# Mixture of experts into attention on one core: layer two's first batch is mixed and normed inside the pass over the experts

## The chip, the cores and the metric

The kernel runs on one core of a Trainium2 chip, as one program. The metric is the device time in microseconds (us), the median over runs. The core's engines have a queue each: TensorE (PE, matrix products and turns, that is transposes through the identity), VectorE (DVE), ScalarE (ACT), GpSimd (POOL) and SyncE (SP, which here only issues DMAs). They meet through semaphores.

## The reference

Eight batches of 512 tokens, 256 wide, pass two layers, float32 throughout:

```python
x = x + attn0(layernorm(x))      # six heads, convolutions, a rotating state scanned over the tokens
x = x + ffn0(layernorm(x))       # sixteen experts, two for each token, and a shared one
x = x + attn1(layernorm(x))      # sixteen heads of 128, causal softmax
x = x + ffn1(layernorm(x))       # gated, 688 wide, weights looked up in a table of sixteen
```

What the change touches is the end of `ffn0` and the start of `attn1`. `ffn0` adds to each token the outputs of its two experts, each times the token's weight for it:

```python
for e in range(E):
    routed = routed + mask[..., e:e + 1] * _swiglu(x, wg[e], wu[e], wd[e])
```

## The kernel before

The first layer runs in four units of two batches. In it each token is given two slots, and GpSimd scatters the normed token to both of them in a DRAM tensor, `tokens_by_expert`, of 80 tiles of 128 slots (`NTILE`), sorted so that each tile belongs to one expert. Slots are given unit by unit, so those of unit 0, which holds batches 0 and 1, lie in the first tiles that were opened; the change reckons with 32.

**The pass over the experts** then takes the 80 tiles one by one. PE works in steps: turn of tile t (`tile_turn`), gate and up of tile t-1 (`tile_gate_up`), turn back of t-2 (`tile_turn_back`), down product of t-3 (`tile_down`). Every fourth step it also reads the numbers of the next four experts into registers. ACT copies each product out of the banks of PSUM and stores the results two tiles at a time (`store_tiles`) into `expert_results`; DVE multiplies gate by up (`tile_product`). Banks 0 and 1 are the turns', 2 and 3 gate and up, 4 and 5 the turn back, 6 and 7 the down product.

Beside its product DVE has a second job in each step: it unpacks the table weights of the second layer's feed-forward part (`unpack_to`). An entry is a comparison in bf16 (`unpack_equal`, equal<-fidx_bf) and a multiply-add (`unpack_add`, fws<-equal), both 128x544. There are 112 of them until the end of the pass, 30 before it starts; the last sixteen, of the late chunk, are left for the first heads of layer two.

**Behind the pass** stands the start of layer two for batch 0, in this order: all results stored (`stored`); eight gathers on GpSimd of the rows that batch 0 needs (`gather`, into `yg`); the mix and the statistics on DVE; the norm (`norm_chain_whole`, `norm_apply`); PE's eight turns of the normed `xn` into banks 6 and 7 (`turn`); ACT's and DVE's split of them into a high and a low part (`layer_norm_high`, `layer_norm_low`, h_high and h_low); and the products of q, k and v for head 0 (`make_qk`, `make_v`). PE fills its wait with turns of the identity (`clock_turns`), 200 and then 20, whose result is not read. Batches 1 to 7 have the same steps spread over the heads of the batch before, and are not touched.

GpSimd's part of the pass is the low half of five weight tiles (`low_qk_weights`, `low_v_weights`, `low_out_weights`), once ACT has copied their high halves in its turns 40 to 48. SP loads the tiles of tokens in pairs, index chunks, two sets of head weights, and x of batches 0 and 1 (`load_x`).

The order of the work on each engine is the order in which this code is written; no scheduler changes it.

## Time and profile before

| | us |
|---|---|
| median of 3 runs | 2196.58 |
| lowest, highest | 2193.62, 2198.37 |
| span of the profiled execution | 2190.4 |
| time of the profiled execution beside its span | not given by the page |
| PE busy | 2123.2 (97%) |
| DVE busy | 1694.3 (77%) |
| ACT busy | 1273.8 (58%) |
| GpSimd busy | 559.2 (26%) |

The span runs from the first to the last instruction of one profiled execution; the runs' times hold what lies around it as well. PE's share counts the fills as work. The shares are means over stages with different limits, so the change has to be read from its own stage, which is the pass (477 to 617 us of the span) and what stands behind it until about 642.

### The profile page before, as it was taken

The page shows a single profiled execution, that of the slowest core. Times are in us where ns is not written, and L with a number is a line of the kernel's source. Part 1 is how long each engine was busy: PE and PEld are TensorE (multiplying, and loading weights), DVE is VectorE, ACT ScalarE, POOL GpSimd, SP SyncE. Part 2 cuts the span into 40 slices and gives each one's busy share as a digit, 9 for nine tenths or more (in the row PEclk, how much of TensorE's full clock was granted, in tenths as well). Part 3 has the DMA queues.
Part 4 walks back from the last instruction along what each step waited for, and adds up shares of the span by engine and source line. Part 5 has one row for each costly group of instructions (what it writes and reads, how often), then busy time and mean ns, then how long its engine had stood idle before and what let it go on. Part 6 is the DMA issues. An engine that isn't in the chain of part 4 may idle for free. (4 is left out here: it accounts for less than half of the span.)

```text
span 2190.4 us, 37661 instructions
## 1 busy us (share of the span) xinstructions
PE 2123.2 (97%) x13038; PEld 1854.3 (85%) x13038; DVE 1694.3 (77%) x4387; ACT 1273.8 (58%) x3487; POOL 559.2 (26%) x604
## 2 busy tenths in 40 slices
PE   6899999979999999999999999999999999999997
PEld 5677777758788999899989989998998999899887
DVE  7998886887767887777876877787687778767775
ACT  5644443226637676666665666666566666656662
POOL 0214333430015323122222312222232222222220
PEclk9999999999999999999999999999999999999999
DMA  9001010436522112112111211211121121111100
GB/s 300 1 1 58 20 46 26 170 121 205 172 68 64 59 51 76 39 52 70 54 40 55 82 39 54 69 54 39 57 80 39 54 68 54 39 58 50 39 20 20
DMA packets 88556, 145.81 MB, mean 67 GB/s; under 512 B 8369, under 2 KB 55857, under 8 KB 88369
## 3 DMA queue, kind: packets, MB, share of 16 engines
q1 hardware_dynamic: 67904, 112.73, 16.1%
q0 software_dynamic: 6144, 16.79, 2.2%
q10 hardware_dynamic: 14320, 13.90, 1.9%
q8 instruction: 106, 1.74, 0.3%
q14 instruction: 82, 0.66, 0.1%
HBM read 105.63 MB, written 37.75 MB: 65 GB/s over the span
## 5 line engine op out<-in xcount | busy, mean ns | idle before, releaser
L1018 ACT ACTIVATE pr<-bank,negmax 128x128 f32<-128x128 f32 (+3 forms) x512 | 263.5, 527 | 196.6 <-DVE negmax L1599 196.6
L653 POOL TENSOR_TENSOR wo_low<-wraw_o,wo_high 128x256 fp32r<-128x256 f32 x128 | 94.5, 738 | 1105.0 <-ACT wo_high L705 1105.0
L1136 DVE TENSOR_TENSOR p_low<-bank,p_high 128x512 fp32r<-128x512 f32 (+2 forms) x384 | 190.2, 551 | 100.6 <-ACT p_high L705 100.0
L705 ACT ACTIVATE p_high<-bank 128x512 fp32r<-128x512 f32 (+2 forms) x384 | 177.4, 497 | 149.9 <-PE bank L2121 149.9
L1599 DVE CUSTOM_DVE_ANT_0 bank<-bank,causal 128x128 f32<-128x128 f32 (+3 forms) x512 | 234.7, 520 | 1.1 <-PE bank L1762 1.1
L1626 DVE SCALAR_TENSOR_TENSOR xs<-bank,rinv,xs 128x256 f32<-128x256 f32 x512 | 211.7, 474 | 1.2 <-PE bank L1762 1.2
L1760 PE MATMUL bank<-h_high,wqk_high 128*128 128x512 f32 x512 | 202.6, 396 | 0.0
L1761 PE MATMUL bank<-h_low,wqk_high 128*128 128x512 f32 x512 | 202.5, 396 | 0.0
L1762 PE MATMUL bank<-h_high,wqk_low 128*128 128x512 f32 x512 | 202.3, 395 | 0.0
L1136 DVE TENSOR_TENSOR z_low<-bank,z_high 128x512 fp32r<-128x512 f32 x128 | 88.4, 691 | 130.8 <-ACT z_high L705 130.3
L643 POOL TENSOR_TENSOR wqk_low<-wraw,wqk_high 128x512 fp32r<-128x512 f32 x128 | 165.6, 1294 | 77.3 <-ACT wqk_high L705 77.3
L2121 PEld LDWEIGHTS bank<-ident,pr 128*128 128x128 f32 x1280 | 147.6, 140 | 18.4 <-ACT pr L1018 1.3
L2121 PE MATMUL bank<-ident,pr 128*128 128x128 f32 x1280 | 160.4, 272 | 1.1 <-ACT pr L1018 1.1
L705 ACT ACTIVATE z_high<-bank 128x512 fp32r<-128x512 f32 x128 | 76.6, 599 | 138.1 <-PE bank L2132 138.1
L1760 PE MATMUL bank<-wv_high,h_high 128*128 128x256 f32 x512 | 154.8, 302 | 0.0
L1760 PE MATMUL bank<-wo_high,z_high 128*128 128x256 f32 x512 | 148.0, 289 | 2.4 <-issue 2.3
L1762 PE MATMUL bank<-wv_high,h_low 128*128 128x256 f32 x512 | 144.5, 282 | 0.0
L1762 PE MATMUL bank<-wo_high,z_low 128*128 128x256 f32 x512 | 144.1, 282 | 0.0
L1761 PE MATMUL bank<-wv_low,h_high 128*128 128x256 f32 x512 | 144.0, 281 | 0.0
L1761 PE MATMUL bank<-wo_low,z_high 128*128 128x256 f32 x512 | 143.8, 281 | 0.0
L1760 PE MATMUL bank<-k_high,q_high 128*128 128x384 f32 (+2 forms) x384 | 140.8, 367 | 0.0
L1760 PE MATMUL bank<-p_high,v_high 128*128 128x512 f32 (+2 forms) x384 | 131.2, 342 | 2.4 <-DVE p_low L1136 2.3
(338 smaller groups left out, 6327.3 us busy)
## 6 DMA issues: line engine op xcount, KB each, us to landing
wraw<-in_wpair SPq DMA_DIRECT2D x64, 512.0 KB, 4.0
wraw<-in_wpair SPq DMA_DIRECT2D x64, 256.0 KB, 4.4
wraw_o<-in_wpair SPq DMA_DIRECT2D x64, 256.0 KB, 2.5
tokens_by_expert<-zero SPq DMA_DIRECT2D x10, 1024.0 KB, 11.2
xt<-tokens_by_expert SPq DMA_DIRECT2D x40, 256.0 KB, 3.3
expert_results<-ey ACTq DMA_DIRECT2D x40, 256.0 KB, 3.7
wres<-in_wexp SPq DMA_DIRECT2D x1, 6144.0 KB, 20.7
xs<-x_between_stages SPq DMA_DIRECT2D x8, 512.0 KB, 4.5
```

The costliest lines, as they stand in the source:

```text
L643: pool.tensor_tensor(low, wraw[r][:, 2 * e * D:2 * (e + 1) * D], high.bitcast(F32), ALU.subtract).then_inc(s_wq, 1)
L653: pool.tensor_tensor(wo2[e][1][:], wraw_o[r][:, e, :], wo2[e][0][:].bitcast(F32), ALU.subtract).then_inc(s_wo, 1)
L705: sc.activation(dst, src, ACT.Copy, scale=scale).then_inc(done, 1)
L1018: ins = sc.activation(pr[:, i, 0:(i + 1) * P], score(i), ACT.Exp, scale=-1.0, bias=negmax[:, i:i + 1], accum_out=rsum[:, i:i + 1])
L1136: v.tensor_tensor(at(parts[1]), src, high_, ALU.subtract).then_inc(done, 1)
L1599: ins = v.tensor_tensor_reduce(score(i), score(i), causal[:, (NT - 1 - i) * P:NT * P], -1.0, -NEG, ALU.add, ALU.min, negmax[:, i:i + 1])
L1626: ins = v.scalar_tensor_tensor(xb[:, i, :], bank[6 + n][:, (i % 2) * D:(i % 2 + 1) * D], rinv[:, i:i + 1], xb[:, i, :], ALU.mult, ALU.add)
L1760: mm(dst, w[0], x[0], start=start, stop=False)
L1761: mm(dst, w[0], x[1], start=False, stop=False)
L1762: return mm(dst, w[1], x[0], start=False, stop=stop)
L2121: ins = pe.transpose(bank[2 + n][:, at:at + P], pr[:, i, j * P:(j + 1) * P], ident[:])
```

## The change

- The gathers of batch 0 wait for 32 stored tiles instead of all, and stand on GpSimd ahead of its five low weights. They read from the first 32 tiles of `expert_results` only.
- The mix of batch 0 goes from DVE to GpSimd: a multiplication of the gathered rows in place and an addition to x, four of each for each of the two experts, each waiting for the one before.
- DVE takes the statistics, the links of the norm and its application in pieces, one behind each tile from tile 56 on (`first_batch`).
- PE turns the normed batch behind the gate and up of the last tile, into banks 0 and 1; ACT and DVE split it in their turn there.
- All fills behind the pass are gone, the 200 and the 20.
- DVE's entries are spread anew over the pass (`entries_until`): 82 instead of 77 fall into it, and in the twelve tiles with a piece of the norm they come half as often. The five late entries behind the pass are gone.
- x of batch 0 is loaded at pair 12 instead of 24. The places of `yg` and of h2 for the even batches in SBUF are exchanged with others, so that they lie outside of what the pass uses. ACT's wait for all stores moves behind its copies of q, k and v.

```diff
-LATE_ENTRIES = 5
+LATE_ENTRIES = 0
+FIRST_TILES = 32
+FIRST_STATS = 56
+FIRST_CHAIN = FIRST_STATS + 4
+FIRST_APPLY = FIRST_CHAIN + 4
...
+            first_tiles_stored(pool)
+            for n in range(2 * NT):
+                gather(0, n)
+            pool.wait_ge(s_x1[0], 16)
+            for c in range(2):
+                for i in range(NT):
+                    if c == 0:
+                        pool.wait_ge(s_yg[i], 32)
+                    linked(pool.tensor_scalar(yg[:, i, c, :], yg[:, i, c, :], wts[:, i, c:c + 1], None, ALU.mult))
+                for i in range(NT - 1):
+                    linked(pool.tensor_tensor(xs[0][:, i, :], xs[0][:, i, :], yg[:, i, c, :], ALU.add))
+                pool.tensor_tensor(xs[0][:, NT - 1, :], xs[0][:, NT - 1, :], yg[:, NT - 1, c, :], ALU.add
+                                   ).then_inc(s_mix, 1)
+                pool.wait_ge(s_mix, c + 1)
             low_qk_weights(0, 0, 0)
...
             stored(pool)
-            for n in range(2 * NT):
-                gather(0, n)
...
+            def first_batch(t):
+                n = t - FIRST_STATS
+                if 0 <= n < NT:
+                    if n == 0:
+                        v.wait_ge(s_mix, 2)
+                    ins = v.bn_stats(stats[:, n, :], xs[0][:, n, :])
...
+                n = t - FIRST_CHAIN
+                if 0 <= n < 4:
+                    norm_chain(2, 0, n)
+                n = t - FIRST_APPLY
+                if 0 <= n < NT:
+                    ins = v.tensor_scalar(xn[:, n, :], xs[0][:, n, :], mv[:, n, 0:1], ry[:, n:n + 1],
+                                          ALU.subtract, ALU.mult)
...
+            def entries_until(t):
+                busy = min(max(t + 1 - FIRST_STATS, 0), FIRST_APPLY + NT - FIRST_STATS)
+                weight = 2 * (t + 1) - busy
+                return (LATE_CHUNK * LUTN - early) * weight // (2 * NTILE - FIRST_APPLY - NT + FIRST_STATS)
...
+            for t in range(NTILE):
+                tile_product(t)
+                unpack_to(early + entries_until(t))
+                first_batch(t)
+            layer_norm_low(2, 0, h2[0], 0)
...
+                if t == NTILE:
+                    turn(2, 0, 0)
```

The first place is PE at the end of the pass. L2040 is gate and up, L2047 the turn back, L2053 the down product, ISA an instruction that reads the expert's number from a register. Before:

```order
L2040 MATMUL bank<-wres,xT 128x256
L2047 MATMUL bank<-ident,eh 128x128
L2053 ISA
L2053 MATMUL bank<-wres,ehT 128x256
L2047 MATMUL bank<-ident,eh 128x128
L2053 ISA
L2053 MATMUL bank<-wres,ehT 128x256
L2053 ISA
L2053 MATMUL bank<-wres,ehT 128x256
L1931 MATMUL bank<-ident 128x128 x200
L2099 MATMUL bank<-ident,xn 128x128 x8
L1931 MATMUL bank<-ident 128x128 x20
```

Now, with the lines of the changed kernel (L2072 is gate and up, L2079 the turn back, L2085 the down product, L2114 the turns of xn):

```order
L2072 MATMUL bank<-wres,xT 128x256
L2114 MATMUL bank<-ident,xn 128x128 x8
L2079 MATMUL bank<-ident,eh 128x128
L2085 ISA
L2085 MATMUL bank<-wres,ehT 128x256
L2079 MATMUL bank<-ident,eh 128x128
L2085 ISA
L2085 MATMUL bank<-wres,ehT 128x256
L2085 ISA
L2085 MATMUL bank<-wres,ehT 128x256
L1792 MATMUL bank<-h_high,wqk_high 128x512
```

The eight turns stand in front of two turns back and three down products, and the first product of layer two directly behind the last of these.

The second place is ACT at the same point: ey is the result of a tile, h_high the high part of the normed batch. Before:

```order
L927 ACTIVATE esg<-bank 128x128
L933 ACTIVATE ehT<-bank 128x128
L940 ACTIVATE ey<-bank 128x256
L944 DMA expert_results<-ey 128x2x256
L933 ACTIVATE ehT<-bank 128x128
L940 ACTIVATE ey<-bank 128x256 x2
L944 DMA expert_results<-ey 128x2x256
L705 ACTIVATE h_high<-bank 128x512 x2
```

Now:

```order
L947 ACTIVATE esg<-bank 128x128
L953 ACTIVATE ehT<-bank 128x128
L960 ACTIVATE ey<-bank 128x256
L725 ACTIVATE h_high<-bank 128x512 x2
L964 DMA expert_results<-ey 128x2x256
L953 ACTIVATE ehT<-bank 128x128
L960 ACTIVATE ey<-bank 128x256 x2
L964 DMA expert_results<-ey 128x2x256
```

The two high copies now stand in front of the last tile's turned copy (ehT), on which PE's last down product waits.

The third place is GpSimd, from the last scatters of the first layer on. Before:

```order
L583 DMA tokens_by_expert<-xm,slots 10240x256 x21
L643 TENSOR_TENSOR wqk_low<-wraw,wqk_high 128x512 x2
L649 TENSOR_TENSOR wv_low<-wraw,wv_high 128x512 x2
L653 TENSOR_TENSOR wo_low<-wraw_o,wo_high 128x256
L669 DMA yg<-expert_results,slots 128x256 x8
```

Now:

```order
L591 DMA tokens_by_expert<-xm,slots 10240x256 x21
L677 DMA yg<-expert_results,slots 128x256 x8
L689 TENSOR_SCALAR yg<-yg,wts 128x256 x4
L691 TENSOR_TENSOR xs<-xs,yg 128x256 x3
L692 TENSOR_TENSOR xs<-xs,yg 128x256
L689 TENSOR_SCALAR yg<-yg,wts 128x256 x4
L691 TENSOR_TENSOR xs<-xs,yg 128x256 x3
L692 TENSOR_TENSOR xs<-xs,yg 128x256
L651 TENSOR_TENSOR wqk_low<-wraw,wqk_high 128x512 x2
```

The gathers and sixteen operations of the mix now stand ahead of the low weights.

## Rows read from the trace of the kernel before

**Rows 1.** The page: its first line, and a row of DMA issues.
```profile
span 2190.4 us, 37661 instructions
...
wraw<-in_wpair SPq DMA_DIRECT2D x64, 512.0 KB, 4.0
```

**Rows 2.** Stretches: us, then busy us (instructions) by engine, granted clock, DMA.
```profile
580.00:600.00 20.00, 20.00 (x109) 16.38 (x108) 15.46 (x38) 13.21 (x49) 0.00 (x0) 1.00 0.56 159
...
621.00:642.00 21.00, 21.00 (x190) 20.66 (x189) 10.73 (x35) 1.09 (x2) 7.49 (x8) 1.00 0.32 102
...
440.00:445.00 5.00, 2.90 (x22) 1.30 (x20) 4.55 (x15) 1.34 (x3) 0.00 (x0) 1.00 0.00 0
```

**Rows 3.** Timeline, 613 to 642: start, us, engine, line, operation [idle before, releaser].
```profile
613.13 1.03 PE L2040 MATMUL bank<-wres,xT 128*128 x4
...
614.50 0.29 DVE L1524 TENSOR_TENSOR eh<-esg,bank 128x128 f32<-128x128 f32 x1
...
616.77 0.39 ACT L940 ACTIVATE ey<-bank 128x256 f32<-128x256 f32 x1 [0.59 <-PE bank L2053]
...
617.18 0.37 ACTq L944 DMA_DIRECT2D expert_results<-ey  x1
...
620.84 1.02 POOL L669 DMA_INDIRECT yg<-expert_results,slots  x1 [57.91 <-DMA expert_results<-ey]
...
636.94 1.38 DVE L1591 TENSOR_SCALAR xn<-xs,mv,ry 128x256 f32<-128x256 f32 x4
...
638.46 1.06 PE L2099 MATMUL bank<-ident,xn 128*128 128x128 f32 x8
...
639.65 1.09 ACT L705 ACTIVATE h_high<-bank 128x512 fp32r<-128x512 f32 x2 [22.49 <-PE bank L2099]
640.27 1.29 DVE L1136 TENSOR_TENSOR h_low<-bank,h_high 128x512 fp32r<-128x512 f32 x2 [1.96 <-ACT h_high L705]
...
641.71 0.47 PE L1760 MATMUL bank<-h_high,wqk_high 128*128 128x512 f32 x1
```

**Rows 4.** Tile xt, whole run: ns min/median/max, first and last start; landing.
```profile
L2034 PE MATMUL bank<-ident,xt x160: 272/273/323, 477.1 to 611.6; 128*128 128x128 f32 x160
...
DMA to landing us min/median/max: 2.7/3.3/5.7
```

**Rows 5.** Timeline, the product and entries on DVE, and the turn back.
```profile
604.78 0.29 DVE L1524 TENSOR_TENSOR eh<-esg,bank 128x128 f32<-128x128 f32 x1 [0.31 <-ACT esg L927]
...
605.90 0.27 PE L2047 MATMUL bank<-ident,eh 128*128 128x128 f32 x1
...
617.81 0.30 DVE L1398 TENSOR_SCALAR equal<-fidx_bf 128x544 bf16<-128x544 bf16 x1
...
618.84 0.29 DVE L1398 TENSOR_SCALAR equal<-fidx_bf 128x544 bf16<-128x544 bf16 x1
```

**Rows 6.** Timeline, 549 to 553, around GpSimd's second weight difference.
```profile
549.11 0.62 ACT L705 ACTIVATE wqk_high<-wraw 128x512 fp32r<-128x512 f32 x1
...
549.81 1.36 POOL L643 TENSOR_TENSOR wqk_low<-wraw,wqk_high 128x512 fp32r<-128x512 f32 x1 [1.98 <-ACT wqk_high L705]
...
550.43 0.90 DVE L1398 TENSOR_SCALAR equal<-fidx_bf 128x544 bf16<-128x544 bf16 x1
...
552.57 0.32 PE L2047 MATMUL bank<-ident,eh 128*128 128x128 f32 x1 [1.06 <-DVE eh L1524]
```

**Rows 7.** Groups on GpSimd: busy us, mean ns, idle before.
```profile
L653 POOL TENSOR_TENSOR wo_low<-wraw_o,wo_high 128x256 fp32r<-128x256 f32 x128 | 94.5, 738 | 1105.0 <-ACT wo_high L705 1105.0
...
L583 POOL DMA_INDIRECT tokens_by_expert<-xm,slots x64 | 65.1, 1017 | 50.4 <-DVE slots L1349 32.4 <-issue 17.8
L669 POOL DMA_INDIRECT yg<-expert_results,slots x64 | 61.2, 957 | 72.7 <-DMA expert_results<-ey 57.9 <-issue 11.4
...
L615 POOL TENSOR_SCALAR shift<-upto,tilenos 128x16 f32<-128x16 f32 x3 | 1.0, 322 | 0.3
```

**Rows 8.** Timeline, the first head: ACT's weight copy.
```profile
657.05 0.62 ACT L705 ACTIVATE wqk_high<-wraw 128x512 fp32r<-128x512 f32 x1
```

More of the change, by code:

```diff
@@ L215, in two_layer_program @@
         fw2 = split("fw2", [P, FW])
-        h2 = [split(f"h2{i}", [P, KD, T]) for i in range(2)]
+        h2_odd = split("h21", [P, KD, T])
         f2 = split("f2", [P, KD, T])
-        yg = sb("yg", [P, NT, 2, D])
         q2 = split("q2", [P, T])
@@ L222, in two_layer_program @@
         v2 = [split(f"v2{i}", [P, NT, 2, DH]) for i in range(2)]
+        yg = sb("yg", [P, NT, 2, D])
+        h2 = [split("h20", [P, KD, T]), h2_odd]
         pr = sb("pr", [P, NT, T])
@@ L384, in stored, with first_tiles_stored @@
                 engine.wait_ge(s_yst[i], 16 * NTILE // 8)
+        def first_tiles_stored(engine):
+            for i in range(4):
+                engine.wait_ge(s_yst[i], 16 * FIRST_TILES // 8)
         def first_layer_over(engine):
@@ L669, in gather @@
                 pool.indirect_dma_start(
-                    yg[:, i, c, :], None, ysort,
+                    yg[:, i, c, :], None, ysort[0:FIRST_TILES * P, :] if b == 0 else ysort,
                     bass.IndirectOffsetOnAxis(ap=slots[:, b * NT + i, c:c + 1], axis=0)).then_inc(s_yg[i], 16)
+            first_tiles_stored(pool)
[12 more added lines that the diff above has]
+                pool.wait_ge(s_mix, c + 1)
             low_qk_weights(0, 0, 0)
@@ L1081, in head @@
                     store_out(b - 1)
-            stored(sc)
-            layer_norm_high(2, 0, h2[0], 6)
             high_q(0)
@@ L1088, in _ @@
             high_v(1, bank[2][:])
+            stored(sc)
             for g in range(NG):
@@ L1518, in _ @@
             v.tensor_copy(expert_row[:], bank[7][0:1, 0:NTILE]).then_inc(s_row, 1)
-            def tile_product(t):
-                v.wait_ge(s_es, t + 1)
-                if t >= 2:
-                    v.wait_ge(s_eu, t - 1)
-                v.tensor_tensor(eh[t % 2][:], esg[t % 2][:], bank[2 + t % 2][:, P:2 * P], ALU.mult).then_inc(s_ea, 1)
-            early = sum(EARLY_ENTRIES)
-            unpack_to(early)
-            for t in range(NTILE):
-                tile_product(t)
-                unpack_to(early + (t + 1) * (LATE_CHUNK * LUTN - LATE_ENTRIES - early) // NTILE)
-            unpack_to(LATE_CHUNK * LUTN)
             def low_q(g):
@@ L2055, in tile_down @@
                    ).then_inc(s_ed, 1)
-            experts = []
-            for t in range(NTILE + 3):
-                if t < NTILE:
-                    tile_turn(t)
-                if 0 <= t - 1 < NTILE:
-                    tile_gate_up(t - 1, experts[t - 1])
-                if t < NTILE and t % NVALUES == 0:
-                    experts += nc.values_load_multi_w_load_instructions(
-                        expert_row[0:1, t:t + NVALUES], engines=(mybir.EngineType.PE,), min_val=0, max_val=NEXP - 1,
-                        bass_reorder=False)[1]
-                if 0 <= t - 2 < NTILE:
-                    tile_turn_back(t - 2)
-                if 0 <= t - 3 < NTILE:
-                    tile_down(t - 3, experts[t - 3])
-            clock_turns(CLOCK_TURNS[5])
-            stored(pe)
             def make_qk(g):
@@ L2093, in make_v, with turn @@
                 ins.then_inc(s_v, 1)
-            def turn(n, b):
+            def turn(n, b, bank0=6):
                 pe.wait_ge(s_xn[n], b + 1)
@@ L2231, in head @@
                     scores(g + 1)
-            turn(2, 0)
-            clock_turns(NORM_TURNS)
+            experts = []
+            for t in range(NTILE + 3):
+                if t < NTILE:
+                    tile_turn(t)
+                if 0 <= t - 1 < NTILE:
+                    tile_gate_up(t - 1, experts[t - 1])
+                if t == NTILE:
+                    turn(2, 0, 0)
+                if t < NTILE and t % NVALUES == 0:
+                    experts += nc.values_load_multi_w_load_instructions(
+                        expert_row[0:1, t:t + NVALUES], engines=(mybir.EngineType.PE,), min_val=0, max_val=NEXP - 1,
+                        bass_reorder=False)[1]
+                if 0 <= t - 2 < NTILE:
+                    tile_turn_back(t - 2)
+                if 0 <= t - 3 < NTILE:
+                    tile_down(t - 3, experts[t - 3])
             make_qk(0)
```

34 lines of the change are left out of this document (16 added, 18 removed).

## The prediction

> **What bounds the kernel now.** I read the page first, for the span, 2190.4 us [rows 1]. The list of the last chain is of no use here, since it names no stretch, so I went to the stretches by time. In the pass over the experts TensorE (PE) is busy for all 20 us of 580 to 600, DVE for 15.5 and GpSimd for none [rows 2]. So PE sets the pace there, and DVE has about a quarter of its time free. Between 621 and 642 us PE is again busy for all 21 us, but with 190 instructions that are the fills (turns of the identity whose result nobody reads): this is a wait painted as work [rows 2]. The timeline says what the wait is for. The last expert product of gate and up starts at 613.13; the last results are stored from 617.18 and have landed by 620.84, when GpSimd's first gather starts; the mix and the norm on DVE go on to the four applications at 636.94; PE turns them at 638.46, ACT and DVE split them, and the first product of layer two starts at 641.71 [rows 3]. The reader is to see one serial chain of 28.6 us from 613.13 to 641.71, in which PE does nothing useful after about 616.7.
>
> **The change, part by part.** *The chain in front of the mix.* It now starts when 32 tiles are stored. PE's turns of the tiles go from 477.1 to 611.6 for 80 tiles, so 1.70 us a tile [rows 4]; tile 35, in whose ACT turn the sixteenth pair's store stands, is at 536.6, the store a little behind it at 537.5. With the 3.7 us from the last store to the gather, 617.18 to 620.84 [rows 3] the gathers start at 541.2. Eight of them at 0.957 and about 0.3 between them [rows 7] are 10.0 us: 551.2.
>
> *The mix on GpSimd.* Eight multiplications and eight additions of 128x256, each waiting for the one before. An addition has its row in the weight difference of that shape, 0.738. The multiplication by a column has none of this width. From below it is 0.32, the row of 16 columns; from above 1.06, that row and the two-input row of 256 columns added. I take 0.84, nearer to the row of the same width. With 0.1 idle behind each (0.3 over three in the row of 16 columns) [rows 7] the mix is 8 x 0.84 + 8 x 0.94 = 14.2 us, to 565.4; the ends are 10.1 and 16.0 us.
>
> *The low weights,* now behind it on GpSimd: four of 1.36 at most [rows 6] and one of 0.74 are 6.2 us, to 571.6. They are wanted at the first product of layer two, 47 us later: no cost.
>
> *The norm in DVE's turns 56 to 67.* PE turns tile 56 at 572.3 and DVE comes to its product two tile steps later, near 575.6. The mix is done 10 us before. Four statistics, sixteen small links and four applications (1.38 together [rows 3]) are about 7 us, spread over twelve tiles in which the new rule gives up half of the unpacking. Of this nothing reaches PE.
>
> *Unpacking.* DVE ends all 112 entries within the pass, five more than before, and eight tiles now have two entries. An entry takes 1.03, a product 0.29 [rows 5]. A double tile is thus 0.2 + 2.06 + 0.1 = 2.4 against the 1.70 of the step: the next product is 0.7 late. A product that starts at 604.78 is read at 605.90 in this rhythm, so about 0.8 is free, and 0.4 a tile is regained. Seven double tiles cost nothing or 0.2 each; that at tile 46 also has the cast of a new chunk and stands within the mix. I put down 0.5 us.
>
> *Contention.* While GpSimd works on a tensor, DVE's comparison in bf16 is held: GpSimd's difference runs from 549.81 for 1.36 us, the comparison that started at 550.43 took 0.90 in place of 0.30, and ended 0.15 behind it [rows 5, 6]. The multiply-add behind it is not held. From 551 to 571 GpSimd is at tensors nearly all the time, so each of some 13 comparisons loses on average a quarter of a microsecond with 0.8 us operations, and 0.5 with the longer ones at the end. A tile then takes 1.34 + 0.3, still below 1.70. I put down 0.5 us for what is left, above all at tile 46.
>
> The Trainium skill ("SBUF — State Buffer", section "SBUF: two separate sides") says the same of the cause: one port pair is shared by DVE and GpSimd, as a lock for a whole instruction, and not as a share of bandwidth. By this rule the held comparisons would wait and the others not, and the trace agrees. The section adds what speaks against this change: a DMA that GpSimd itself issues cannot write its descriptors while DVE holds the pair, 620 ns alone and about 3100 ns beside a DVE copy. With 3.1 us for each gather the mix would end at 580, and the sum would be 18 instead of 22. The row that bears on it, GpSimd's scatters, with DVE's comparisons beside part of them, has a mean of 1.017 against 0.957 of the gathers [rows 7], which shows little of it; I keep the rows' price.
>
> *The tail.* PE's last gate and up end at 614.16. Eight turns behind them (1.06 [rows 3]) end at 615.1, the turn back and down product of older tiles at 615.7. ACT's queue then has a result of 0.39, ending at 616.1, the two high halves (1.09, to 617.2), and one more short copy, 617.5; only then can PE do the last down product, which ends near 618.4. DVE's product of the last tile is at 614.50, its two entries end at 616.8, and the two low halves (1.29) behind the high ones end at 618.2 [rows 3]. Both paths meet at 618.4, where before there stood 641.71: **23.3 us**. The fills are gone, and PE stands idle for about 2 us at 616 to 618. Between 440 and 445 PE is busy for 2.90 of 5.00 us and the granted clock stays at 1.00, its upper level, 2.4 GHz [rows 2], so I put nothing on it.
>
> *What is late next.* The last result now leaves ACT near 618.8, the stores have landed by 622.5, and the next weight load, which waits for them as the first gather did at 620.84, is issued at 622.9. It feeds ACT's copy that stood at 657.05 and will stand at 633.8: 10.9 us for a load of 512 KB, which takes 4.0 by the page's row for these loads [rows 1, 8]. ACT's own wait for the stores now stands behind its copies of q, k and v, which need two rounds of products after 618.4 first; 622.5 is close to that, and I put nothing on it. *The earlier load of x* at the pair 12: the tile loads have landed in 5.7 us at worst [rows 4], and the next tile pair is asked for six tiles, 10 us, ahead. Its half megabyte and the megabyte of gathers are hidden by that.
>
> **Sum.** 23.3 saved in the tail, 1.0 given back in the pass: 22.3 us. The span would be 2168.1. The page gives no time for the profiled execution beside its span; the span is 6.2 us under the median of the runs, 2196.58, and I carry this over: 2174.3 us.
>
> **Rivals.**
> *Contention eats the pass.* If each of 13 comparisons lost the full 0.6 seen, that is 7.8 us; about 0.35 a tile is free, 4.2 over twelve tiles, and 0.8 once: 2.8 us. There are two PE idles of 1.0 already now near GpSimd's work, one at 552.57 in front of a turn back; I read them as ACT's, whose weight copy at 549.11 pushes the tile's own copy back just before PE reads its expert numbers [rows 6]. If they are GpSimd's, one or two more come: up to 4.8 in all. The price over the 1.0 already counted is 1.8 to 3.8, and the time 2176 to 2178. For it speaks the held row; against it that most of a tile's DVE work isn't held.
>
> *The mix is late.* DVE would stand at tile 56 with the last products behind it, and the PE loop with it. From 575.6 on each microsecond costs one. With 3.1 us a gather it is 4.4: 2178.7. By the rows it ends 10 us earlier.
>
> *Slower than before.* The same wait at tile 56, if GpSimd's operations got through only once in a DVE hold each. It decides from a mix that ends at 575.6 + 22.3 = 598, or 2.9 us for each of sixteen operations instead of 0.89; with 3.5 it is 10 us more, 2206. The weight difference of 512 columns, beside DVE's work, took 1.36 [rows 6], less than twice the 0.738 mean of 256 columns over the whole program, so GpSimd is hardly held.
>
> *The change doesn't do what it says:* the first product waits for something else that the fills hid, the weights or the stores, and stays near 641: 2197. I find nothing that is not ready by 623.
>
> **How the numbers follow.** The forecast has 0.73, contention 0.14, the late mix 0.06, no effect 0.02, slower 0.03, and 0.02 is a gain above 24.5 us. The forecast's own range is 2171.5 to 2176, with 1.5 us for the spread of the runs (2193.62 to 2198.37). To hold 8 in 10 I take in contention and most of the late mix, and the run spread below: 2171 to 2179.5. A measurement tells about 0.2%, 4.4 us, from no change: faster 0.95, same 0.02, slower 0.03.
>
> **What would show it.** In the changed kernel's profile: eight gathers near 541; sixteen GpSimd operations of 0.5 to 0.9 ending by 567; comparisons of up to 0.9 among them; no DVE wait for xs at its first statistics near 576; the eight turns of xn directly behind the last gate and up, near 614 to 616; the first product of layer two near 619, and the later stages shifted by the same amount. The two 1.0 idles of PE near 552 and 560 stay if they are ACT's. Wrong would be: a DVE wait for GpSimd at tile 56, several new PE idles between 550 and 572, the clock below 1.00 behind 616, or a wait for a weight load in the first head.

## The result and the profile after

| | before | changed |
|---|---|---|
| median, us | 2197.47 (4 runs, 2193.62 to 2199.59) | 2177.61 (4 runs, 2175.25 to 2182.67) |
| span of the profiled execution | 2190.4 | 2173.5 |

The ratio is 0.9916, with a 95% interval of 0.9904 to 0.9928: the change makes the kernel faster by 0.84%. The forecast was 2174.3, with a range of 2171 to 2179.5. The span of the profiled execution fell by 16.9 us where 22.3 were forecast, so a quarter of the gain is missing, and the study is about that quarter. The median came nearer to its forecast than the span did; how that came about stands under the sum at the end.

The page of the changed kernel, its first line and the busy times of the engines:

```profile
span 2173.5 us, 37227 instructions
PE 2102.6 (97%) x12818; PEld 1830.9 (84%) x12818; DVE 1694.2 (78%) x4379; ACT 1274.5 (59%) x3487; POOL 575.1 (26%) x620
```

PE's busy time is 20.6 us less, in the main the fills; GpSimd's is 15.9 more, the mix. DVE's sum is the same within 0.1 though the mix has left it: a DVE instruction that GpSimd's work holds up ("held" below) shows a longer time and counts as busy for all of it. A better first question than the totals is in which stage the time went. I cut the span at four starts: PE's first turn of a tile, the last gate and up, the first product of layer two, and ACT's first z_high (the high half of the first attention output).

| stage | before | changed | difference | forecast |
|---|---|---|---|---|
| up to the first turn | 477.1 | 477.4 | +0.3 | 0 |
| the pass, to the last gate and up | 136.03 | 141.23 | +5.2 | +1.0 |
| from there to layer two's first product | 28.58 | 5.08 | -23.5 | -23.3 |
| from there to z_high | 16.41 | 17.44 | +1.0 | 0 |
| the rest | 1532.28 | 1532.35 | +0.1 | 0 |

Up to the first turn both kernels do the same work there, but that stretch takes from 477 to 486 us in the executions below. The last stage, the rest, takes from 1532.1 to 1533.9 us in them. So single spans can't be compared to a microsecond; the three stages between can. The pass of the changed kernel took 141.23, and 141.07 and 141.15 in two other executions with the same pass.

**The tail.** The timeline of the changed kernel around the last gate and up: start, us, engine, line, operation, and in brackets the idle time before it with its releaser, as in [rows 3].

```profile
618.63 1.03 PE L2072 MATMUL bank<-wres,xT 128*128 x4
...
619.50 1.04 PE L2114 MATMUL bank<-ident,xn 128*128 128x128 f32 x8
...
621.87 0.60 ACT L725 ACTIVATE h_high<-bank 128x512 fp32r<-128x512 f32 x1
622.28 1.28 DVE L1157 TENSOR_TENSOR h_low<-bank,h_high 128x512 fp32r<-128x512 f32 x2
...
622.78 0.69 PE L2085 MATMUL bank<-wres,ehT 128*128 x2 [0.99 <-ACT ehT L953]
...
623.71 0.47 PE L1792 MATMUL bank<-h_high,wqk_high 128*128 128x512 f32 x1 [0.23 <-DVE h_low L1157]
```

The reader is to see that both paths of the forecast are there. PE waits 0.99 us for ACT's late ehT, and then 0.23 for DVE's low halves. Put on the forecast's clock (gate and up at 613.13), the first product stands at 618.21; 618.4 was forecast.

**Behind the tail.** ACT's rows of the changed kernel, and then of the one before, around its first exponentials of layer two:

```profile
632.86 1.28 ACT L1040 ACT_TABLE_LOAD   x1 [2.54 <-DVE negmax L1607]
634.15 0.37 ACT L1040 ACTIVATE pr<-bank,negmax 128x128 f32<-128x128 f32 x1
```

```profile
648.33 1.28 ACT L1018 ACT_TABLE_LOAD   x1
650.78 0.37 ACT L1018 ACTIVATE pr<-bank,negmax 128x128 f32<-128x128 f32 x1 [1.17 <-DVE negmax L1599]
```

Before, ACT loaded the table of the exponential while it would have waited for the maxima anyway, and still waited 1.17 us behind the load. Now the load begins only when the maxima are there, and its 1.28 us are all on the path.

**GpSimd in the pass.** Its timeline in the changed kernel, from the first gather on:

```profile
540.90 0.98 POOL L677 DMA_INDIRECT yg<-expert_results,slots  x1 [69.27 <-DMA expert_results<-ey]
...
550.69 4.80 POOL L689 TENSOR_SCALAR yg<-yg,wts 128x256 f32<-128x256 f32 x4
555.57 2.35 POOL L691 TENSOR_TENSOR xs<-xs,yg 128x256 f32<-128x256 f32 x3
...
559.18 4.16 POOL L689 TENSOR_SCALAR yg<-yg,wts 128x256 f32<-128x256 f32 x4
563.43 2.70 POOL L691 TENSOR_TENSOR xs<-xs,yg 128x256 f32<-128x256 f32 x3
566.20 0.73 POOL L692 TENSOR_TENSOR xs<-xs,yg 128x256 f32<-128x256 f32 x1
567.01 2.92 POOL L651 TENSOR_TENSOR wqk_low<-wraw,wqk_high 128x512 fp32r<-128x512 f32 x2
569.89 3.03 POOL L657 TENSOR_TENSOR wv_low<-wraw,wv_high 128x512 fp32r<-128x512 f32 x2
572.88 1.21 POOL L661 TENSOR_TENSOR wo_low<-wraw_o,wo_high 128x256 fp32r<-128x256 f32 x1
```

The gathers start within 0.3 us of the forecast. The mix runs from 550.69 to 566.9 (forecast 551.2 to 565.4). A row of four multiplications takes 4.80 and 4.16 us with the gaps between them; one alone takes 0.92 to 1.38, 1.05 on the mean. GpSimd is at tensors without a gap from 550.69 to 574.1.

**What DVE and PE do meanwhile.** The timeline of the changed kernel beside the low weights:

```profile
568.83 1.67 DVE L1429 SCALAR_TENSOR_TENSOR fws<-equal,luts,fws 128x544 f32<-128x544 bf16 x1
...
570.43 0.28 DVE L1751 TENSOR_TENSOR eh<-esg,bank 128x128 f32<-128x128 f32 x1
570.63 1.17 DVE L1419 TENSOR_SCALAR equal<-fidx_bf 128x544 bf16<-128x544 bf16 x1
570.76 0.33 PE L2079 MATMUL bank<-ident,eh 128*128 128x128 f32 x1 [1.02 <-DVE eh L1751]
...
571.83 1.67 DVE L1429 SCALAR_TENSOR_TENSOR fws<-equal,luts,fws 128x544 f32<-128x544 bf16 x1
...
573.75 0.33 PE L2079 MATMUL bank<-ident,eh 128*128 128x128 f32 x1 [1.01 <-DVE eh L1751]
```

An entry is an unheld comparison of 0.30 and a multiply-add of 0.79 elsewhere (the comparison in [rows 5]). Here both are held, 1.17 and 1.67, and with the product a tile takes DVE 3.0 us. PE's turns back stand 2.99 us apart, at 570.76 and 573.75. The product itself, which reads one input out of PSUM, takes its 0.28.

**PE's other idles in the pass.** The turns back of the changed kernel that had over 0.4 us in front of them, the two above left out:

```profile
546.13 0.32 PE L2079 MATMUL bank<-ident,eh 128*128 128x128 f32 x1 [0.56 <-issue]
...
554.11 0.33 PE L2079 MATMUL bank<-ident,eh 128*128 128x128 f32 x1 [1.08 <-DVE eh L1751]
...
562.00 0.32 PE L2079 MATMUL bank<-ident,eh 128*128 128x128 f32 x1 [0.99 <-issue]
...
599.54 0.33 PE L2079 MATMUL bank<-ident,eh 128*128 128x128 f32 x1 [0.44 <-issue]
```

The idles at 554 and 562 are the two of before ([rows 6] has the first). Those at 546 and 599 are new, and no GpSimd instruction on a tensor runs at either. I laid the turns back of both kernels beside each other and took the difference of their times tile by tile. Beyond the later start of the pass it grows by 0.4 in the first turns, where an entry now stands in turn 0; by 0.8 at 546; by 0.7 over 565.8 and 567.8, beside the mix's additions; by 2.7 from 570.8 to 575.6, beside and just behind the low weights; and by 0.6 at 599. These are 5.2 us, the difference of the stages.

### The profile page after: what moved, and what is told of

It is laid out like the page before. It is cut to its first block and busy times, and to the rows that moved or that the text cites. A ratio compares the mean times of both kernels' runs of the same rounds, so it can differ in the third digit from the quotient of the medians.

```text
span 2173.5 us, 37227 instructions
## 1 busy us (share of the span) xinstructions
PE 2102.6 (97%) x12818; PEld 1830.9 (84%) x12818; DVE 1694.2 (78%) x4379; ACT 1274.5 (59%) x3487; POOL 575.1 (26%) x620
## 3 DMA queue, kind: packets, MB, share of 16 engines
q1 hardware_dynamic: 67904, 112.73, 16.2%
```

## The experiments

The theory: the missing time is (a) entries held beside the low weights and the mix, 3 to 3.5 us; (b) entries that make a product late just before a turn in which PE reads expert numbers into registers, about 1.5 to 2 with the entry in turn 0; (c) the table load behind the stores' wait, 1.0. The rival for (a) is that the gathers' DMA or the placement of the entries slows the pass, and GpSimd's tensor work only stands beside it.

**1. The wait for the stores one step earlier.** The forecast put ACT's wait at nothing. The order of instructions shows what it became: the table load is made directly in front of the first exponential, and waits that stand between the last copy and the exponential come ahead of the load. ACT's row in the order, changed kernel, then kernel before:

```
L1040 ACT_TABLE_LOAD [waits tiles_stored3,tiles_stored2,score_max_bank,tiles_stored1]
L1018 ACT_TABLE_LOAD
```

The exponential now needs five waits, four for the stores and one for the maxima. It keeps one of the stores'; the other four, the one for the maxima among them, have gone ahead of the load. The edit:

```diff
             high_v(0, bank[5][:])
-            high_v(1, bank[2][:])
             stored(sc)
+            high_v(1, bank[2][:])
```

> The changed kernel with one edit: ACT's wait for all stores stands in front of the second copy of v instead of behind it. In the changed kernel the table load of the exponentials starts at 632.86, behind the first row maxima, and the first exponential at 634.15; the lead at the first product of layer two is 18.0 us against the kernel before, and 17.0 from the first head's z on. Theory: the wait for the stores, put directly ahead of the exponentials, drags the wait for the row maxima in front of the table load, so 1.28 us of loading are no longer hidden. Then here the load stands before 631.7, the first exponential 1.1 us behind the first row maximum, and the span is 1.0 us shorter, 2172.5. Rival: the load is late because ACT itself is late there (stores landing at 626); then the span stays at 2173.5 and the load stays behind the maxima.

The load then stands in the order with no wait at all, and ACT's timeline reads:

```profile
634.35 1.28 ACT L1040 ACT_TABLE_LOAD   x1
...
636.80 0.37 ACT L1040 ACTIVATE pr<-bank,negmax 128x128 f32<-128x128 f32 x1 [1.17 <-DVE negmax L1607]
```

From layer two's first product to z_high it took 16.52 us instead of 17.44, and the 1.17 of before is back. The span, 2178.0, isn't the 2172.5 expected: its pass began at 481.4 instead of 477.4, and its last stage took 1533.85 instead of 1532.35, a length that kernels without this edit reach too (1533.74 in experiment 5). (c) holds by its stage: 0.9 us.

**2. Low weights ahead of the gathers.** ACT's five copies go to turns 20 to 30, and GpSimd's five differences stand in front of the gathers:

```diff
+            low_qk_weights(0, 0, 0)
...
+            low_out_weights(0, 0, 0)
             first_tiles_stored(pool)
...
-                if t in (40, 42):
-                    high_qk_weights((t - 40) // 2)
+                if t in (20, 22):
+                    high_qk_weights((20, 22).index(t))
```

> The changed kernel with the five weight copies on ACT in turns 20, 22, 24, 28, 30 instead of 40 to 48, and GpSimd's five low weights ahead of the gathers, so that they run one at a time and not back to back behind the mix. The count of copies just before a register read is the same. Theory: GpSimd's operations of 1.3 to 1.5 us back to back hold both the comparison (1.17 instead of 0.30) and the multiply-add (1.67 instead of 0.79) of an entry, so two steps of 2.99 us stood in the pass between 567.8 and 573.8; here these two steps are 1.63 to 1.85 long and the first product of layer two is 2.3 to 2.6 us earlier (span 2170.9 to 2171.2); the two idles of 1.0 move to about 518 to 532. Rival: the two long steps come from DVE's own load, double entries and the cast; then they stay, and the span is within 0.5 us of 2173.5.

The pass took 138.64, 2.6 less, and both steps of 3 us are gone. The two idles of 1.0 have moved with ACT's copies, to 524.08 and 538.83. The differences now come singly, and DVE's and GpSimd's timeline shows what one alone does:

```profile
518.11 1.69 POOL L651 TENSOR_TENSOR wqk_low<-wraw,wqk_high 128x512 fp32r<-128x512 f32 x1 [41.67 <-ACT wqk_high L725]
...
518.79 1.17 DVE L1419 TENSOR_SCALAR equal<-fidx_bf 128x544 bf16<-128x544 bf16 x1
...
520.00 0.79 DVE L1429 SCALAR_TENSOR_TENSOR fws<-equal,luts,fws 128x544 f32<-128x544 bf16 x1
```

The comparison is held and the multiply-add isn't, since GpSimd is done by then. That is what stood in [rows 6] too, and it is why the forecast took the multiply-add for one that can't be held.

**3. ACT's weight copies off the register reads.** The copies of turns 42 and 46 go to 41 and 45:

```diff
-                if t in (40, 42):
-                    high_qk_weights((t - 40) // 2)
-                if t in (44, 46):
-                    high_v_weights((t - 44) // 2)
+                if t in (40, 41):
+                    high_qk_weights((40, 41).index(t))
+                if t in (44, 45):
+                    high_v_weights((44, 45).index(t))
```

> The changed kernel with ACT's weight copies in turns 40, 41, 44, 45, 48 instead of 40, 42, 44, 46, 48: none of them now stands two turns behind a register read's turn. Theory: the two PE idles of 1.0 us at 554.1 and 562.0 (552.57 and 560.47 before the change) come from a copy that delays the tile's own copy just ahead of the four expert numbers being read; both vanish and the span is 2.0 to 2.3 us shorter, near 2171.3. Rival: they are GpSimd's, through DVE's held entries; then both stay and the span does not move by more than 0.4.

The pass took 139.28, 1.95 less, just under the 2.0 to 2.3 expected. The first idle is gone: PE's turns back pass its place in steps of 1.6 to 1.8 (the row of 553.97 and the one behind it are a turn with a register read):

```profile
552.34 0.27 PE L2079 MATMUL bank<-ident,eh 128*128 128x128 f32 x1
...
553.97 0.31 PE L2079 MATMUL bank<-ident,eh 128*128 128x128 f32 x1
...
555.80 0.27 PE L2079 MATMUL bank<-ident,eh 128*128 128x128 f32 x1
```

At the second place an idle of 0.42 stays, one turn later, at 563.23, behind the turn that has two entries and the cast of a new chunk beside the mix. So the two idles were ACT's and not GpSimd's, though the profile names DVE as releaser of one of them, and 0.4 at the second place is DVE's. DVE's product is only the next in the row: it waits for the copies behind ACT's late one.

**4. No mix.** The gathers stay; the sixteen operations of the mix are left out, so that batch 0 goes on without its experts' outputs:

```diff
-            for c in range(2):
...
+            for i in range(NT):
+                pool.wait_ge(s_yg[i], 32)
+            pool.sem_inc(s_mix, 2)
```

> The changed kernel without the mix of batch 0: the gathers stay, GpSimd's eight multiplications and eight additions are left out (so batch 0 goes on without its experts' outputs), the low weights follow at once. Theory: the mix costs the pass the slow steps at 565.8 and 567.8 (0.7 us) and pushes the low weights into one block (2.5 us); without it these come one by one as before the change, and the first product of layer two is 3.0 to 3.4 us earlier (span 2170.1 to 2170.5); what stays against the pass before is 0.7 at its start, 0.8 at 546.1 and 0.6 at 599.5. Rival: the loss in the pass is DVE's own, entries and norm pieces; then the span moves by less than 1 us.

The pass took 137.97, 3.3 less. Without the mix the low weights are differences with gaps, as ACT delivers them. The gathers and the entries are still there, so neither the gathers' transfers nor the place of the entries alone costs these 3.3; (a) holds against its rival.

**5. Entries off the register reads.** No entry in turn 0; two entries only in turns of the form 4k+1 (9, 13, 17, 25, 37, 45, 53, 69, 77), and in the twelve turns of the norm one in six of them:

```diff
+            doubles = (9, 13, 17, 25, 37, 45, 53, 69, 77)
+            ones = (57, 58, 59, 61, 65, 66)
...
             def entries_until(t):
...
+                return sum(entries_of(n) for n in range(t + 1))
```

> The changed kernel with only DVE's entries spread otherwise: none in turn 0 as before the change, and the two-entry turns at 9, 13, 17, 25, 37, 45, 53, 69, 77, that is always just after a turn of number 4k, and the entries beside the norm pieces in turns 57, 58, 59, 61, 65, 66; 82 in all as before. Theory: every fourth turn PE's queue reads four expert numbers into registers and has no time to spare there, so a late product only costs when it is the one of turn 4k+1; this explains 0.8 us at 546.1 (behind the double turn 36) and 0.6 at 599.5 (behind turn 64 with cast and application); both idles vanish and the pass from first turn to last gate and up is 139.0 to 139.8 us long against 141.2. Rival: any late product costs, wherever the double turns stand; then the idles only move and the pass is 140.8 us or longer.

The pass took 139.59, 1.5 less than the 141.07 of the changed kernel on the same chip, and the idles at 546 and 599 are gone. A new one came: the double turn 45 falls into the mix's additions with the cast of a new chunk, and PE waits 1.46 us for its product at 568.19. Behind the low weights stands another of 0.61, at 584.67.

**6 and 7. All four together, with the mix on GpSimd and on DVE.** Both have the edits of 1, 2, 3 (weight copies in turns 20, 21, 24, 29, 28) and 5. The second takes the mix off GpSimd; DVE does it as one instruction for each gathered block, in eight turns that read no registers and hold no norm:

```diff
+            MIXES = (45, 46, 48, 49, 50, 52, 53, 54)
...
+                    ins = v.scalar_tensor_tensor(xs[0][:, i, :], yg[:, i, c, :], wts[:, i, c:c + 1], xs[0][:, i, :],
+                                                 ALU.mult, ALU.add)
```

> All four edits together: stores' wait in front of the second copy of v, weight copies on ACT in turns 20, 21, 24, 28, 29 (none two turns before a register read's turn end), low weights ahead of the gathers, entries as in the run of the entries alone. If the four causes are separate, their gains add: pass 134.3 to 135.2 us (141.2 less 2.6, 2.0 and 1.5 to 2.2), first product to first z 16.5 instead of 17.4, so 7.0 to 7.8 us below the changed kernel on the same chip, and 0.9880 to 0.9890 of the kernel before. If they overlap (the same slack counted more than once) the gain is under 6 us.

> As the run with all four edits, but the mix of batch 0 done by DVE as before the change, one of its eight operations (0.48 us) in each of the turns 45, 46, 48, 49, 50, 52, 53, 54, and GpSimd left with the gathers. Theory: GpSimd's operations hold the entries beside them, which costs the pass about what DVE's own eight would (4 us of DVE work, most of it in free time), so the pass is within 0.7 us of that with the mix on GpSimd. Rival: DVE is the bound in these turns, and each operation adds its 0.48 less 0.3 of free time to the pass: 1.5 us longer or more. Other rival: GpSimd's hold is what still costs, and without it the pass is 0.8 us shorter or more.

> The changed kernel itself once more, beside the others on one chip: pass 141.2 us, first product to first z 17.4, ratio to the kernel before 0.9916 within its interval. It gives the spread of the stage lengths between executions, expected at 0.1 us in the pass and up to 5 us in where the pass starts.

All three ran on one chip, with the kernel before at 2196.39 (9 runs):

| | median (lowest, highest), us | ratio to before, 95% | pass | to z_high |
|---|---|---|---|---|
| changed | 2180.77 (2179.97, 2181.12) | 0.9927 (0.9914 to 0.9941) | 141.07 | 17.42 |
| all four, mix on GpSimd | 2174.67 (2169.53, 2175.96) | 0.9894 (0.9875 to 0.9913) | 136.88 | 16.50 |
| all four, mix on DVE | 2172.67 (2172.38, 2175.32) | 0.9890 (0.9875 to 0.9906) | 135.56 | 16.49 |

By their medians the mended kernels are 6.1 and 8.1 us faster than the changed one. Of that the pass and the stage behind the tail carry 5.1 and 6.4, and another 0.3 is in the tail, 4.82 us in both; the rest lies in the spread of the stages that no edit touches. The sum of the four gains, 7.0 to 7.8, was missed. With the mix on DVE the pass is 0.5 shorter than in the kernel before, though it holds more entries and the whole mix; but that kernel still had its two idles of 1.0. It is 1.3 shorter than with the mix on GpSimd, where within 0.7 was expected: the second rival held, by which GpSimd's hold is what still costs.

With the mix on GpSimd the pass missed its expected 134.3 to 135.2 by 1.7 at least. That lies in two places. The first is new in both mended kernels: the copies of turns 20 and 21 come so close that GpSimd's first two differences, from 516.90 to 518.30 and from 518.52 on, follow each other, and a tile's two instructions are held again, 0.94 and 1.88. Two steps of PE take 2.20 and 2.22 instead of 1.63, 1.2 us in all:

```profile
518.49 1.88 DVE L1429 SCALAR_TENSOR_TENSOR fws<-equal,luts,fws 128x544 f32<-128x544 bf16 x1
518.52 1.27 POOL L651 TENSOR_TENSOR wqk_low<-wraw,wqk_high 128x512 fp32r<-128x512 f32 x1 [0.22 <-ACT wqk_high L725]
...
520.62 0.33 PE L2087 MATMUL bank<-ident,eh 128*128 128x128 f32 x1 [0.41 <-DVE eh L1759]
```

The second is the turn of experiment 5's new idle. DVE, GpSimd and PE there in the kernel with all four edits:

```profile
560.61 2.70 POOL L696 TENSOR_TENSOR xs<-xs,yg 128x256 f32<-128x256 f32 x3
...
561.53 1.19 DVE L1429 SCALAR_TENSOR_TENSOR fws<-equal,luts,fws 128x544 f32<-128x544 bf16 x1
...
562.64 0.96 DVE L1401 CAST fidx_bf<-fidxs 128x544 bf16<-128x544 int32 x1
563.38 0.80 POOL L697 TENSOR_TENSOR xs<-xs,yg 128x256 f32<-128x256 f32 x1
563.64 0.70 DVE L1419 TENSOR_SCALAR equal<-fidx_bf 128x544 bf16<-128x544 bf16 x1
564.28 4.37 POOL L694 TENSOR_SCALAR yg<-yg,wts 128x256 f32<-128x256 f32 x4
564.38 0.67 DVE L1426 TENSOR_SCALAR fws<-equal,luts 128x544 f32<-128x544 bf16 x1
564.97 0.27 DVE L1759 TENSOR_TENSOR eh<-esg,bank 128x128 f32<-128x128 f32 x1
...
565.30 0.33 PE L2087 MATMUL bank<-ident,eh 128*128 128x128 f32 x1 [1.83 <-DVE eh L1759]
```

Four held instructions in a row, 3.5 us, and PE waits 1.83. With the mix on DVE the same cast, comparison and first multiplication take 0.44, 0.30 and 0.51, the mix's own instruction 0.48, and PE waits 0.29:

```profile
564.97 0.44 DVE L1390 CAST fidx_bf<-fidxs 128x544 bf16<-128x544 int32 x1
565.44 0.30 DVE L1408 TENSOR_SCALAR equal<-fidx_bf 128x544 bf16<-128x544 bf16 x1
565.78 0.51 DVE L1415 TENSOR_SCALAR fws<-equal,luts 128x544 f32<-128x544 bf16 x1
566.19 0.48 DVE L1725 SCALAR_TENSOR_TENSOR xs<-yg,wts,xs 128x256 f32<-128x256 f32 x1
...
566.93 0.33 PE L2091 MATMUL bank<-ident,eh 128*128 128x128 f32 x1 [0.29 <-DVE eh L1763]
```

**8 to 11. Could the mix stay on GpSimd at no cost?** Three kernels asked whether the 1.83 is the double turn with its cast. Number 8 has edits 1 to 3 with the changed kernel's entries; 9 has all four with doubles at 33 and 41 in place of 37 and 45; 10 is the changed kernel with no entries in turns 48 to 51. The ninth was run again, as the eleventh.

> The version with all four edits, but with the entries spread as in the changed kernel. Theory: the entries' edit gained 1.5 us alone and lost it again in the sum, because its double turn 45 meets the cast of a chunk and GpSimd's mix (one idle of 1.83 us); then the three other edits add up, 141.1 less 2.6 and 2.0, and the pass is 136.3 to 136.8 us, as long as with all four. Rival: the edits of low weights and weight copies overlap; then the pass is 137.5 us or longer.

> The version with all four edits, with the double turns 37 and 45 moved to 33 and 41, so that no double turn stands beside the mix and its cast turn. Theory: the idle of 1.83 us came from the double turn with cast beside GpSimd's multiplications; without it the pass is 135.0 to 135.6 us, the same as with the mix on DVE (135.56). Rival: GpSimd's hold costs the same whatever stands beside it; then the pass stays at 136.5 us or above.

> The changed kernel with only the entries moved: none in turns 48 to 51, where the low weights run back to back on GpSimd, and two in turns 13, 22, 31, 41 instead; GpSimd's and ACT's work as in the changed kernel. Theory: GpSimd's block costs only by holding the entries' two instructions; with none beside it the two long steps (2.99 us each) are 1.63 to 1.85 long though the block stays, and the pass is 138.3 to 139.0 us. Rival: GpSimd holds the products as well, or ACT or PE; then the long steps stay in part and the pass is 140 us or longer.

> The version with the double turns at 33 and 41 once more, since the last three runs had a halt of several microseconds near 550 to 562 on all engines that no edit touches, and their pass lengths can't be used. As before: theory, the idle of 1.83 us in the version with all four edits came from its double turn 45 with the cast beside GpSimd's multiplications, and the pass is 135.0 to 135.6 us without it. Rival: GpSimd's hold costs the same whatever stands beside it, and the pass is 136.5 us or longer. The disturbed run points between the two: the idle was gone, but the steps beside the additions were 1.8 to 2.1 us long, 1.0 us over in sum, which would make 136.0.

| | time, us | kernel before, same chip | pass |
|---|---|---|---|
| three mended, entries as changed | 2186.09 | 2204.04 | 144.35 |
| all mended, double moved | 2182.67 | 2204.04 | 140.38 |
| no entries beside low weights | 2187.62 | 2204.04 | 147.94 |
| all mended, double moved, again | 2178.57 (4 runs) | 2204.92 (7 runs) | 140.76 |

None of these pass lengths can be used. Each of the four executions has some microseconds between 548 and 565 in which PE, DVE and ACT slow down at once, beside the later of GpSimd's eight gathers, which go on, most of them at their 0.94 to 0.95 us each. No edit touches that place. Stretches of the first of them (us, then busy us of PE, PE's weight loads, DVE, ACT and GpSimd, PE's granted clock, DMA share, GB/s):

```profile
555.00:560.00 5.00, 2.64 (x11) 1.58 (x11) 0.82 (x4) 0.94 (x3) 3.78 (x5) 1.00 0.66 220
560.00:565.00 5.00, 3.77 (x10) 2.61 (x11) 2.25 (x5) 2.04 (x8) 4.60 (x6) 0.53 0.41 133
```

In the five microseconds from 555 on DVE and ACT did less than 1 us of work each, while PE's granted clock was still 1.00, its upper level of 2.4 GHz; only in the stretch behind them it was 0.53, near the lower level of 1.2 GHz. What halts them I can't tell: it came in these four executions, on two chips, and in none of the ten others of this study, which have the same gathers or, before the change, none there. The fourth row's median does carry a ratio, 0.9889 (0.9863 to 0.9915), the same as that of the other mended kernels within the intervals; whether its three other executions had the halt isn't known. In its profiled execution the old 1.83 us idle is gone, and three turns beside the mix's additions are 1.8 to 2.1 us apart. Experiments 2 and 3, which had no halt, say more. There a double turn with the same cast met the mix as well, but mostly beside its multiplications: the cast took 0.77, the comparisons 0.46 and 0.28, the second multiply-add 0.80, and PE's idle was 0.44 and 0.42. So the double turn and its cast alone don't make 1.83; they made 1.46 and 1.83 where they stood beside the additions. Whether a mix on GpSimd can be had for less than the 1.3 us by which DVE's is ahead stays open. The tenth kernel shows one thing by the way: its pass was shifted, so the low weights met a double turn with entries after all, and a PE idle of 2.51 us stood at 578.01, behind comparisons of 1.17 and 1.36 and multiply-adds of 1.67 and 1.66.

## Why the prediction was right, and where a quarter of the gain went

**The chain in front of the mix**: right. Gathers at 540.90 (541.2). They take 0.94 to 0.98 us each with 0.30 between, beside DVE's comparisons and multiply-adds; in some later kernels one or two of the eight took 1.46 or 1.47. The late mix, a rival with 0.06, was decided by this: DVE never waits for xs at tile 56, and the mix ends about 15 us before its statistics. The Trainium skill ("SBUF — State Buffer", section "SBUF: two separate sides") has about 3100 ns for such an issue beside a DVE copy. No gather here comes near that.

**The mix on GpSimd**: 16.2 us where 14.2 were forecast, and 16.0 was the upper end. The multiplication was mis-sized: 1.05 on the mean, and I had taken 0.84 in a bound of 0.32 to 1.06. That is 1.7 of the 2.0 us; the additions, 0.82 on the mean instead of 0.738, are most of the rest. It cost nothing by its end, but it put the low weights behind it 1.5 us later.

**The norm in DVE's turns**: nothing of it reached PE by its length. One place has a cost by position: tile 64's turn has the cast of a chunk, an entry and an application, its next product is late, and PE reads registers in the turn behind it: 0.6 us at 599.

**Unpacking**: "Seven double tiles cost nothing or 0.2 each", 0.5 us in all. The sum was short by about 1.4. It counted how long a double tile delays DVE and what is regained, and treated all turns alike. They aren't. In every fourth turn PE's queue also reads the experts' numbers into registers, and a step there takes 1.80 to 1.85 us with nothing late at all; a product late by 0.8 in front of it cost 0.8 and wasn't regained. That the register reads are what takes the slack there is read from the order of the instructions; experiments 3 and 5 moved the work and not the reads. Experiment 5 gives 1.5 for taking entries off those turns and turn 0, net of its new idles of 1.46 and 0.61.

**Contention**: this is the step that failed, in the sentence "The multiply-add behind it is not held". It is: 0.95, 1.19 and up to 1.67 us instead of 0.79, in eight of the eleven that start between 550.8 and 574.3. I had read one entry beside one GpSimd instruction [rows 6]; experiment 2 shows the same picture beside single instructions, and the changed kernel another beside a row of them. Where GpSimd's operations follow each other, both instructions of an entry lose, and with the 512-wide differences, 1.5 us each there, a tile takes DVE 3.0. How much is lost goes by GpSimd's operation. Over all fourteen profiled executions of this case, a multiply-add that started at least 0.3 us before the end of such an operation took 1.66 to 1.70 beside a difference of 512 (15 of them), 1.13 to 1.20 beside an addition or difference of 256 (45), and 0.78 to 0.95 beside a multiplication (49); the product never took more than 0.29. I put down 0.5; the mix and the low weights behind it cost 3.3 (experiment 4), of which the low weights' place alone is up to 2.6 (experiment 2). The Trainium skill ("SBUF — State Buffer", section "SBUF: two separate sides") has a half of its lock rule that I left out: besides the fast modes, a DVE instruction with two inputs in SBUF also needs the shared ports against a GpSimd instruction that reads SBUF. By it the multiply-add is held, and the product, with one input in PSUM, isn't; the trace agrees with both, 1.67 against 0.79, and 0.28. Beside the multiplications, 0.92 us long at least in the changed kernel, it loses 0.16 at most, so there the traces don't show a lock for a whole instruction, as I had cited it. That rule and the low weights' 6 us without a gap would have given the rival *Contention eats the pass* more than its 0.14. The measured 2177.61 lies in its 2176 to 2178 and above the forecast's own 2171.5 to 2176, and of the several new idles between 550 and 572 that were named as a sign of being wrong one did come, at 570.76, with another just behind, at 573.75. Its mechanism is not the whole of the loss, though: about 3.3 of 5.2.

**The two idles of 1.0**: read rightly as ACT's. Experiment 3 moves two copies by one turn each and gains 1.95 us; the first idle is gone, and 0.42 of DVE's stays at the second.

**The tail**: right, 23.5 against 23.3, and by the two paths that were named. The granted clock between 620 and 625 was 1.00, its upper level of 2.4 GHz, with PE busy for 3.77 of the 5 us; before that stretch PE had been busy for all of 615 to 620.

```profile
615.00:620.00 5.00, 5.00 (x30) 4.29 (x30) 3.85 (x9) 3.31 (x12) 0.00 (x0) 1.00 0.30 105
620.00:625.00 5.00, 3.77 (x19) 2.50 (x18) 3.48 (x7) 2.47 (x7) 0.00 (x0) 1.00 0.20 67
```

**What is late next**: the weights were in time, with the load issued at 626.47 and its copy by ACT at 639.93, in which no wait stands. ACT's own wait, on which I "put nothing", cost 1.0, and not by its length. The stores had landed before the maxima were ready, but the wait for the maxima had come ahead of a table load of 1.28 us together with it, and so the load left the gap in which it had been free (experiment 1).

**The sum.** 23.5 saved; 5.2 given back in the pass, 1.0 behind the tail, and 0.3 in a later start of the pass with 0.1 at the end: 16.9. The forecast had 23.3 and 1.0. The misses are contention, 2.8, register turns and turn 0, about 1.4, and the table load, 1.0.

**From the span to the time**: here luck helped. The forecast added 6.2 us, the distance from the span to the median before. In the changed kernel that distance is 4.1; the span is that of one execution and the median that of several, whose times lie up to 7.4 us apart. So the span missed its forecast by 5.4 us and the time its own by 3.3. With the 6.2 the measured span would have made 2179.7, just outside the range of 2171 to 2179.5.

## What to carry to other kernels

Where a helper engine's work is laid beside another's, ask of each of the pair's instructions whether it can be held, and count back-to-back operations as a row of their own: one held instruction is regained in a loop with slack; a tile in which both instructions of an entry are held is not. A loop has turns without slack (here those that read registers), and added or late work belongs in the others; two copies moved one turn earlier were worth 1.95 us together. But ask what follows from the new place: two copies in turns 20 and 21 put GpSimd's differences next to each other, and that cost 1.2 us. Look at what an edit leaves between a wait and the next instruction of the compiled order, for a table load or another preparation that was free may now stand behind the wait.

## What the runs showed of the hardware beyond that

- DVE's multiply-add of 128x544 with both inputs in SBUF took 0.79 us alone and up to 1.88 beside GpSimd's operations; the cast from int32 0.44 alone and 0.52 to 0.97; the product with an input in PSUM 0.27 to 0.29 in either case.
- In the changed kernel a GpSimd multiplication of 128x256 by a column took 0.92 to 1.38 us, an addition of two such tensors 0.73 to 1.09 beside the same DVE work.
- A load of ACT's table took 1.28 us, and four of the five waits of the exponential behind it stood ahead of it.
- The first 480 us of the kernel took from 477 to 486 us in executions of kernels that are the same there.
